# Stacked query and key rows: three stores in final order and one load of 96 rows, in place of one store and six loads of 16 rows

## The chip, the core and the metric

The kernel runs on one core of one Trainium2 chip. The metric is the device time of one execution in microseconds (us). Five engines work side by side, each with its own queue of instructions: TensorE (PE: matmuls; PEld: its weight loads), VectorE (DVE), ScalarE (ACT), GpSimd (POOL) and SyncE (SP). SP computes nothing here. It waits for semaphores and issues all transfers (DMAs), which sixteen DMA engines carry out. Engines and transfers wait for one another through semaphores only; a transfer adds 16 to its semaphore when it has landed.

## The reference, cut to what is computed

One Perceiver block over `x` [4, 256, 256] with a context [4, 4096, 256]. `ln` is a layer norm without weights.

```python
def reference(x, ctx, ...):
    x = x + xattn(ln(x), ctx)      # one head of width 256 over 4096 context tokens
    x = x + attn(ln(x))            # 16 heads of width 16, causal, three heads re-weighted by region
    x = x + soft_moe(ln(x))        # 64 experts with 32 slots each
    return x

# attn, per batch element and head h:
qkv = h @ c_attn_w + c_attn_b
scores = q @ k.T / sqrt(16)        # causal mask, softmax
attn = softmax(scores)             # heads 0 to 2: times 1.6 in one third of the tokens, normalised again
out = (attn @ v) @ c_proj_w + c_proj_b
```

The change lies in how `q` and `k` of the second step get from their projection to the score matmuls.

## The kernel before

Three blocks of code follow one another: `cross_attention`, `self_attention` and `soft_moe`. At the end of a block all five engines meet before any of them starts on the next one (line 202 is the head of the first).

**Why rows are stacked.** A projection value is split into three bf16 parts: high (ACT, `high_part`), middle (DVE forms the rest, ACT rounds it, `middle_part`) and low (POOL, L407 in cross-attention and L1073 in self-attention; semaphore `low_g`). The kernel sums six products of parts for a score. A head is only 16 wide, so it lays six rows of parts for each of the 16 dimensions on 96 partitions (`STACK` = 6, `ROWS` = 96), and one matmul over 96 partitions (L1163 and L1171, in `score`) sums all six products. `Q_STACK` and `K_STACK` name the part in each of the six places. Heads 0 to 2 have three more rows, which DVE fills.

**Eight stages.** `qk_stage(s)` gives for s = 0 to 7 a tile of 128 output columns (query tile 0, key tile 2, query tile 1, key tile 3) and a half of the tokens (s // 4: 512 tokens, two batch elements). The projection leaves the parts of one stage on 128 partitions, [128, 3, 512] bf16, with partition p = 8 i + h for dimension i and head h of the tile. The score matmuls want dimension i on the partition and head h along it. The parts go through DRAM for this:

- `store_parts(s)` waits for `low_g` of the stage and stores all three parts in one transfer of 384 KB (L119), in pieces of 1 KB.
- `stack_rows(s)` waits until that store has landed (`parts_out0` or `parts_out1`) and issues six loads (L128) of 16 partitions, 128 KB each. Each partition receives 8 KB, which lie together in DRAM. They add to `rows_in{s}`.

**The order on SP** is written out by hand. In `cross_attention` it is store 0, loads 0, store 1, loads 1, store 2, loads 2, store 3, and then the end of the block; no stage's instructions are put before those of the stage ahead. In `self_attention` SP issues loads 3, then store 4, loads 4, store 5, loads 5, store 6, loads 6, store 7, loads 7, and after these the load of `phi_w` (L1044, 2 MB) for the third step. Every transfer goes through SP's one queue.

**Who waits.** PE waits for `rows_in` 0 and 1 as it enters self-attention, and for 2 and 3 before `score(2, 0)`. The main loop of self-attention runs over i = 0 to 15 (four batch elements times four groups of four heads). Iteration i transposes the probabilities of group i, mixes group i - 1, and computes the first part of the scores of group i + 3. `rows_in` 4 and 5 are waited for at i = 5, 6 and 7 at i = 7, and the load of `phi_w` at i = 8, where `transpose_phi` (L1227) begins. The projections of stages 4 to 7 stand in the loop at i = 0 to 3, and their low parts in POOL's iterations 1 to 4. The buffers of parts are different ones for each stage, so no engine waits for a store to land except SP.

Of the kernel before, what the change touches and what calls it, by code (L numbers as in the profile page):

```python
# [9 lines left out]
P = 128  # L10
# [4 lines left out]
DH = D // P  # L15
# [8 lines left out]
BF16 = mybir.dt.bfloat16  # L24
# [3 lines left out]
NH, HD, GH = 16, 16, 4  # L28
# [1 line left out]
HPH = P // HD  # L30
CG = 2 * HD
NPART = 3
Q_STACK = (0, 0, 1, 0, 2, 1)
K_STACK = (0, 1, 0, 2, 0, 1)
STACK = len(Q_STACK)
ROWS = STACK * HD
FOCUSED = 3
LOG_FOCUS = math.log(1.6)
HALF = B * S // 2
# [61 lines left out]
def qk_stage(s):  # L101

    return QK_TILES[s % 4], slice(s // 4 * HALF, (s // 4 + 1) * HALF)


def heads_of(rows):
    return slice((rows % DH) * HPH, (rows % DH + 1) * HPH)
# [7 lines left out]
def store_parts(sp, kept, qk_dram, parts, s):  # L115

    rows, _ = qk_stage(s)
    sp.wait_ge(kept.sem["low_g"], s + 1)
    sp.dma_start(qk_dram[rows, s // 4].rearrange("c p t -> p c t"), parts).then_inc(kept.sem[f"parts_out{s % 2}"], 16)  # L119


def stack_rows(sp, kept, qk_dram, q_rows, k_rows, s):

    rows, _ = qk_stage(s)
    sp.wait_ge(kept.sem[f"parts_out{s % 2}"], 16 * (s // 2 + 1))
    for r in range(STACK):
        to, part = (q_rows, Q_STACK[r]) if rows < DH else (k_rows, K_STACK[r])
        sp.dma_start(to[r * HD:(r + 1) * HD, heads_of(rows), :],  # L128
                     qk_dram[rows, s // 4, part].rearrange("(i h) t -> i h t", i=HD)).then_inc(kept.sem[f"rows_in{s}"], 16)


def focus_factor(dve, nc, kept, ident):
# [833 lines left out]
def self_attention(nc, x_sb, x_stats, x_mv, x_ve, x_rstd, ident, kept, disp, ones, qk_dram, phi_w):  # L966
# [4 lines left out]
    with ExitStack() as st:  # L971
        def sb(name, shape, dt=F32):
            return st.enter_context(nc.sbuf_tensor(name, shape, dt))
# [8 lines left out]
        parts = sb("qk_parts", [P, AHEAD, NPART, HALF], BF16)  # L982
# [43 lines left out]
        rows_in = [kept.sem[f"rows_in{k}"] for k in range(8)]  # L1026
# [85 lines left out]
        def _(pe):  # L1112
# [64 lines left out]
            def transpose(G):  # L1177
                g = G % NG
                pe.wait_ge(norm_g, 2 * G + 2)
                at_least(pe, pT_a, G)  # L1180
                at_least(pe, pT_v, 2 * G)
                for h in range(GH):
                    to = psT[h // 2][:, (h % 2) * S:(h % 2 + 1) * S]
                    nc.tensor.transpose(to[:, 0:P], eA[:, g, h, :], ident[:])
                    last = nc.tensor.transpose(to[:, P:S], eB[:, g, h, 0:P], ident[:])
                    if h % 2:
                        last.then_inc(t_mm, 1)
                for h in range(GH):
                    last = nc.tensor.transpose(psT[2][:, h * P:(h + 1) * P], eB[:, g, h, P:S], ident[:])
                last.then_inc(t_mm, 1)  # L1190
# [34 lines left out]
            def transpose_phi(k):  # L1225
                for j in range(4):
                    last = nc.tensor.transpose(psX[:, j * P:(j + 1) * P],  # L1227
                                               phi_nat[:, k // 2 * 4 + j, k % 2 * P:(k % 2 + 1) * P], ident[:])
                last.then_inc(phi_mm, 1)

            for s in range(2):
                pe.wait_ge(rows_in[s], 16 * STACK)
            for part in range(3):
                score(0, part)
            transpose_attended()
# [4 lines left out]
            for part in range(3):  # L1240
                score(1, part)
            for s in (2, 3):
                pe.wait_ge(rows_in[s], 16 * STACK)
            score(2, 0)
            for i in range(GROUPS):
                if i + 2 < GROUPS:
                    score(i + 2, 1)
                    score(i + 2, 2)
                if i == 0:
                    pe.wait_ge(attT_a, B)  # L1250
                    pe.wait_ge(values_v, 2)
                    pe.wait_ge(xadd_v, QT * B)
                transpose(i)
                if i == 0:
                    transpose_second()
                if i == 8:
                    pe.wait_ge(phi_in, 16)
                    pe.wait_ge(out_v, 1)
                    transpose_phi(0)
                if i == 9:  # L1260
                    pe.wait_ge(phi_a, 1)
                    transpose_phi(2)
                if i in (11, 12):
                    pe.wait_ge(phi_a, i - 9)
                    transpose_phi(2 * i - 18)
                if i + 3 < GROUPS:
                    if i == 5:
                        for s in (4, 5):
                            pe.wait_ge(rows_in[s], 16 * STACK)
                        pe.wait_ge(frows_v, 10)  # L1270
                    if i == 7:
                        for s in (6, 7):
                            pe.wait_ge(rows_in[s], 16 * STACK)
                    score(i + 3, 0)
                if i == 1:
                    pe.wait_ge(values_v, 3)
                if i:
                    mix(i - 1)
                if i == 0:
                    pe.wait_ge(h2T_a, B)  # L1280
                    project_qk(4)
                if i in (1, 2, 3):
                    pe.wait_ge(rest_v, i + 4)
                    project_qk(i + 4)
                if i == 4:
                    pe.wait_ge(rest_v, 8)
                    project_v(3)
                if i == 5:
                    pe.wait_ge(values_v, 4)
                    project_out(0)  # L1290
                if i == 8:
                    pe.wait_ge(phi_v, 1)
                    transpose_phi(1)
                if i == 9:
                    pe.wait_ge(phi_v, 2)
                    project_out(1)
                if i == 10:
                    pe.wait_ge(out_v, 2)
                    transpose_phi(3)
                if i in (11, 12):  # L1300
                    pe.wait_ge(phi_v, i - 8)
                    transpose_phi(2 * i - 17)
                if i == 13:
                    pe.wait_ge(phi_a, 4)
                    project_out(2)
                if i >= GROUPS - 2:
                    pe.wait_ge(exp_a, 2 * GH * GROUPS)
                    transpose_normed(i - GROUPS + 2)
# [689 lines left out]
def perceiver_block(nc, x, ctx, Wq, bq, Wk, bk, Wv, bv, Wo, bo, c_attn_w, c_attn_b, c_proj_w, c_proj_b,  # L1998
                    phi_w, phi_b, expert_w, expert_b, out):
    SL = phi_w.shape[0]  # L2000
    with ExitStack() as st:
        x_sb = st.enter_context(nc.sbuf_tensor("x_sb", [P, TT, D], F32))
        x_stats = st.enter_context(nc.sbuf_tensor("x_stats", [P, TT, 6], F32))
        x_mv = st.enter_context(nc.sbuf_tensor("x_mv", [P, TT, 2], F32))
        x_ve = st.enter_context(nc.sbuf_tensor("x_ve", [P, TT], F32))
        x_rstd = st.enter_context(nc.sbuf_tensor("x_rstd", [P, TT], F32))
        ident = st.enter_context(nc.sbuf_tensor("ident", [P, P], F32))
        front = st.enter_context(nc.sbuf_tensor("front", [P, DH * SL], F32, side="right"))
        back = st.enter_context(nc.sbuf_tensor("back", [P, DH * SL], F32, side="right"))
        phib = st.enter_context(nc.sbuf_tensor("phib", [P, SL], BF16, side="right"))  # L2010
        wide = st.enter_context(nc.sbuf_tensor("wide", [P, TT * D], F32, side="right"))
        turned = st.enter_context(nc.sbuf_tensor("turned", [P, DH, B * S], F32, side="right"))
        bank = [st.enter_context(nc.psum_tensor(f"ps{i}", [P, 512], F32)) for i in range(8)]
        qk_dram = nc.dram_tensor("qk_parts_dram", (2 * DH, 2, NPART, P, HALF), BF16).ap()
        phi_dram = nc.dram_tensor("phi_parts_dram", (NPART, SL), BF16).ap()
        with ExitStack() as until_moe:
            kept = carried_tensors(nc, until_moe, bank, front, back, phib, wide, turned)
            cross_attention(nc, x_sb, x_stats, x_mv, ident, kept, x, ctx, Wq, bq, Wk, bk, Wv, bv, Wo, bo,
                            c_attn_w, c_attn_b, c_proj_w, c_proj_b, phi_b, qk_dram, phi_dram)
            disp = st.enter_context(nc.sbuf_tensor("disp", [P, TT, SL], F32))  # L2020
            ones = st.enter_context(nc.sbuf_tensor("ones", [P, P], BF16))
            self_attention(nc, x_sb, x_stats, x_mv, x_ve, x_rstd, ident, kept, disp, ones, qk_dram, phi_w)
        soft_moe(nc, x_sb, x_stats, x_mv, x_ve, x_rstd, ident, kept, disp, ones, expert_w, expert_b, out)
# [22 lines left out]
```

## Time and profile before

| | |
|---|---|
| time, median of 3 runs (all) | 675.2 us (675.18, 675.20, 678.64) |
| time of the profiled execution | 674.29 us |
| its span, from the first instruction to the last | 672.5 us |
| busy: PE, PEld, DVE, ACT, POOL | 608.6, 474.9, 397.4, 347.9, 249.5 us |
| mean granted TensorE clock | 0.962 of full |
| moved by DMA | 52.48 MB, 78 GB/s over the span |

The profiled execution lies 0.9 us below the median, and 1.8 us of it lie outside the span. Positions below are us from the start of the span. The shares of busy time are means over three blocks with different limits; the timelines and the stretches between 279 and 374 us are those in which this change's transfers run.

### The profile page before, as it was taken

The page shows a single profiled execution, that of the slowest core. Times are in us where ns is not written, and L with a number is a line of the kernel's source. Part 1 is how long each engine was busy: PE and PEld are TensorE (multiplying, and loading weights), DVE is VectorE, ACT ScalarE, POOL GpSimd, SP SyncE. Part 2 cuts the span into 40 slices and gives each one's busy share as a digit, 9 for nine tenths or more (in the row PEclk, how much of TensorE's full clock was granted, in tenths as well). Part 3 has the DMA queues.
Part 4 walks back from the last instruction along what each step waited for, and adds up shares of the span by engine and source line. Part 5 has one row for each costly group of instructions (what it writes and reads, how often), then busy time and mean ns, then how long its engine had stood idle before and what let it go on. Part 6 is the DMA issues. An engine that isn't in the chain of part 4 may idle for free. (4 is left out here: it accounts for less than half of the span.)

```text
span 672.5 us, 10468 instructions
## 1 busy us (share of the span) xinstructions
PE 608.6 (91%) x3740; PEld 474.9 (71%) x3740; DVE 397.4 (59%) x797; ACT 347.9 (52%) x1051; POOL 249.5 (37%) x206
## 2 busy tenths in 40 slices
PE   6998999999999998988985899899999876689998
PEld 5887999899989987866663674344448643358887
DVE  4756566666667664626774786968883578244000
ACT  2545444444444536633894783488885457741210
POOL 1442252232223243124586571333644159155000
PEclk9989999999999998998898999999999996789999
DMA  7223122112211210275188104000007048660000
GB/s 258 64 95 110 33 67 91 64 48 93 66 64 47 80 48 2 56 137 91 40 142 170 58 2 126 1 0 1 0 0 169 20 132 274 200 209 8 17 17 23
DMA packets 37000, 52.48 MB, mean 78 GB/s; under 512 B 4307, under 2 KB 31827, under 8 KB 36182
## 3 DMA queue, kind: packets, MB, share of 16 engines
q1 hardware_dynamic: 36950, 51.82, 28.2%
q8 instruction: 30, 0.49, 0.3%
q14 instruction: 20, 0.16, 0.1%
HBM read 47.60 MB, written 4.21 MB: 77 GB/s over the span
## 5 line engine op out<-in xcount | busy, mean ns | idle before, releaser
L379 POOL TENSOR_TENSOR ctx_lo<-front,ctx_hi 128x1024 fp32r<-128x1024 f32 x32 | 76.3, 2388 | 157.8 <-DVE ctx_hi L800 135.9
L485 PE MATMUL ps<-ctx_hi,pT_hi 128*128 128x256 f32 x256 | 75.5, 295 | 0.7 <-DVE pT_lo L815 0.7
L815 DVE TENSOR_TENSOR pT_lo<-ps,pT_hi 128x512 fp32r<-128x512 f32 x64 | 41.2, 686 | 56.1 <-ACT pT_hi L673 56.1
L487 PE MATMUL ps<-ctx_hi,pT_lo 128*128 128x256 f32 x256 | 72.6, 283 | 0.0
L486 PE MATMUL ps<-ctx_lo,pT_hi 128*128 128x256 f32 x256 | 72.5, 283 | 0.0
L650 ACT CAST ctxT_hi<-ps 128x512 fp32r<-128x512 f32 x64 | 34.5, 593 | 64.2 <-PE ps L442 64.2
L1711 PE MATMUL ps<-front,turned 128*128 128x512 f32 x128 | 63.5, 618 | 0.0
L1825 ACT ACTIVATE comb<-comb,cneg 128x64 f32<-128x64 f32 x160 | 62.8, 399 | 0.0
L1803 PE MATMUL ps<-front,comb 128*128 128x256 f32 x256 | 57.9, 387 | 0.0
L1658 POOL TENSOR_TENSOR disp<-disp,dinv 128x512 f32<-128x512 f32 x32 | 33.5, 1048 | 57.1 <-DVE dinv L1905 57.1
L1803 PEld LDWEIGHTS ps<-front,comb 128*128 128x128 f32 x256 | 49.5, 195 | 7.2 <-issue 0.4
L673 ACT CAST pT_hi<-ps 128x512 fp32r<-128x512 f32 x64 | 34.3, 588 | 36.0 <-PE ps L467 36.0
L485 PEld LDWEIGHTS ps<-ctx_hi,pT_hi 128*128 128x128 f32 x256 | 49.2, 192 | 1.4 <-DVE pT_lo L815 1.1
L486 PEld LDWEIGHTS ps<-ctx_lo,pT_hi 128*128 128x128 f32 x256 | 49.3, 193 | 0.1
L487 PEld LDWEIGHTS ps<-ctx_hi,pT_lo 128*128 128x128 f32 x256 | 49.1, 192 | 0.0
L792 DVE TENSOR_TENSOR ctxT_lo<-ps,ctxT_hi 128x512 fp32r<-128x512 f32 x64 | 41.2, 685 | 7.5 <-ACT ctxT_hi L650 7.1
L454 PE MATMUL ps<-ctxT_hi,qk_hi 128*128 128x512 f32 x128 | 43.0, 418 | 2.8 <-issue 2.0
L1669 POOL TENSOR_TENSOR comb<-comb,cinv 128x512 f32<-128x512 f32 x32 | 39.9, 1271 | 15.1 <-DVE cinv L1918 15.1
L1405 DVE TENSOR_REDUCE nmax<-ps 128x2 f32<-128x512 f32 (+1 forms) x48 | 31.9, 672 | 15.6 <-PE ps L1173 8.2
L454 PE MATMUL ps<-ctxT_lo,qk_hi 128*128 128x512 f32 x128 | 40.2, 396 | 0.0
L454 PE MATMUL ps<-ctxT_hi,qk_lo 128*128 128x512 f32 x128 | 40.2, 395 | 0.0
L467 PE MATMUL ps<-ident,wide 128*128 128x128 f32 x256 | 34.5, 278 | 3.7 <-ACT wide L664 3.5
(227 smaller groups left out, 1390.5 us busy)
## 6 DMA issues: line engine op xcount, KB each, us to landing
front<-in_ctx_dram SPq DMA_DIRECT2D x32, 512.0 KB, 3.3
back<-in_L_ffn_expert_w_dram SPq DMA_DIRECT2D x11, 1024.0 KB, 5.5
turned<-in_L_ffn_expert_w_dram SPq DMA_DIRECT2D x5, 1024.0 KB, 5.4
disp<-qk_parts_dram SPq DMA_DIRECT2D x24, 128.0 KB, 4.3
disp<-in_L_ffn_phi_w_dram SPq DMA_DIRECT2D x1, 2048.0 KB, 11.0
front<-in_L_ffn_expert_b_dram SPq DMA_DIRECT2D x4, 512.0 KB, 10.5
qk_parts_dram<-scores SPq DMA_DIRECT2D x4, 384.0 KB, 5.7
front<-qk_parts_dram SPq DMA_DIRECT2D x12, 128.0 KB, 4.4
```

Of the source, the lines that this page charges most:

```text
L379: nc.gpsimd.tensor_tensor(ctx_lo[:, cols], ctx_in_sb[:, c % SLOTS, :], ctx_hi[:, cols].bitcast(F32), ALU.subtract).then_inc(split_g, 1)
L454: last = nc.tensor.matmul(pS[q][:], a[:, dh, q * P:(q + 1) * P], k[:, c % 2, dh, :], start=step == 0, stop=step == 5)
L467: last = nc.tensor.transpose(to[q][:, j * P:(j + 1) * P], probs[:, c % 2, q, j * P:(j + 1) * P], ident[:])
L485: nc.tensor.matmul(pO[q][:, 0:D], pT_hi[:, c % 2, q, cols], hi, start=c == 0 and j == 0, stop=False)
L486: nc.tensor.matmul(pO[q][:, 0:D], pT_hi[:, c % 2, q, cols], lo, start=False, stop=False)
L487: last = nc.tensor.matmul(pO[q][:, 0:D], pT_lo[:, c % 2, q, cols], hi, start=False, stop=c == NCH - 1 and j == J - 1)
L792: nc.vector.tensor_tensor(ctxT_lo[:, c % 2, dh, :], ctx_banks(c, alone)[dh][:], ctxT_hi[:, c % 2, dh, :].bitcast(F32), ALU.subtract).then_ ...
L815: nc.vector.tensor_tensor(pT_lo[:, c % 2, q, :], probs_banks(c, alone)[q][:], pT_hi[:, c % 2, q, :].bitcast(F32), ALU.subtract).then_inc(p ...
L1669: nc.gpsimd.tensor_tensor(part, part, cinv[:, c, :].unsqueeze(1).broadcast_to([P, EB, NS]), ALU.mult).then_inc(cmul_g, 1)
L1711: last = nc.tensor.matmul(psL[u % 4][:], hT[:, c, t * P:(t + 1) * P], phiT[:, c, cols], start=False, stop=c == DH - 1)
L1803: last = nc.tensor.matmul(psY[t][:, 0:HID], comb[:, t, s * P:(s + 1) * P], mixed[:, s, :], start=s == 0, stop=s == ST - 1)
L1825: nc.scalar.activation(column, column, ACT.Exp, bias=cneg[:, c, p:p + 1], accum_out=csum[:, c, p:p + 1]).then_inc(cslot_a, 1)
```

## The change

The scratch tensor in DRAM has six slots per stage instead of three, in the order in which the rows are wanted. `store_parts` now issues three stores on the same queue. For a query tile they hold the high part three times, the middle part twice and the low part once (a source that repeats by a step of zero). For a key tile they hold parts 0 to 2, 0 to 1 and 0. The three stores hold 384, 256 and 128 KB, 768 KB in all, again in pieces of 1 KB. `stack_rows` waits for all three and issues one load of 96 partitions, 768 KB, in place of six. The order of the six places is a new one, but the six products are the same ones. PE's waits ask for 16 instead of 96. Nothing else is changed: the order of the stages on SP, the buffers and the work of the other engines are the same.

```diff
--- before.py
+++ after.py
@@ -30,9 +30,7 @@
 HPH = P // HD
 CG = 2 * HD
 NPART = 3
-Q_STACK = (0, 0, 1, 0, 2, 1)
-K_STACK = (0, 1, 0, 2, 0, 1)
-STACK = len(Q_STACK)
+STACK = NPART * (NPART + 1) // 2
 ROWS = STACK * HD
 FOCUSED = 3
 LOG_FOCUS = math.log(1.6)
@@ -116,17 +114,22 @@
 
     rows, _ = qk_stage(s)
     sp.wait_ge(kept.sem["low_g"], s + 1)
-    sp.dma_start(qk_dram[rows, s // 4].rearrange("c p t -> p c t"), parts).then_inc(kept.sem[f"parts_out{s % 2}"], 16)
+    first = 0
+    for r in range(NPART):
+        count = NPART - r
+        part = parts[:, r:r + 1, :].broadcast_to([P, count, HALF]) if rows < DH else parts[:, 0:count, :]
+        sp.dma_start(qk_dram[rows, s // 4, first:first + count].rearrange("r p t -> p r t"),
+                     part).then_inc(kept.sem[f"parts_out{s % 2}"], 16)
+        first += count
 
 
 def stack_rows(sp, kept, qk_dram, q_rows, k_rows, s):
 
     rows, _ = qk_stage(s)
-    sp.wait_ge(kept.sem[f"parts_out{s % 2}"], 16 * (s // 2 + 1))
-    for r in range(STACK):
-        to, part = (q_rows, Q_STACK[r]) if rows < DH else (k_rows, K_STACK[r])
-        sp.dma_start(to[r * HD:(r + 1) * HD, heads_of(rows), :],
-                     qk_dram[rows, s // 4, part].rearrange("(i h) t -> i h t", i=HD)).then_inc(kept.sem[f"rows_in{s}"], 16)
+    sp.wait_ge(kept.sem[f"parts_out{s % 2}"], 16 * NPART * (s // 2 + 1))
+    to = q_rows if rows < DH else k_rows
+    sp.dma_start(to[0:ROWS, heads_of(rows), :],
+                 qk_dram[rows, s // 4].rearrange("r (i h) t -> (r i) h t", i=HD)).then_inc(kept.sem[f"rows_in{s}"], 16)
 
 
 def focus_factor(dve, nc, kept, ident):
@@ -1229,7 +1232,7 @@
                 last.then_inc(phi_mm, 1)
 
             for s in range(2):
-                pe.wait_ge(rows_in[s], 16 * STACK)
+                pe.wait_ge(rows_in[s], 16)
             for part in range(3):
                 score(0, part)
             transpose_attended()
@@ -1240,7 +1243,7 @@
             for part in range(3):
                 score(1, part)
             for s in (2, 3):
-                pe.wait_ge(rows_in[s], 16 * STACK)
+                pe.wait_ge(rows_in[s], 16)
             score(2, 0)
             for i in range(GROUPS):
                 if i + 2 < GROUPS:
@@ -1266,11 +1269,11 @@
                 if i + 3 < GROUPS:
                     if i == 5:
                         for s in (4, 5):
-                            pe.wait_ge(rows_in[s], 16 * STACK)
+                            pe.wait_ge(rows_in[s], 16)
                         pe.wait_ge(frows_v, 10)
                     if i == 7:
                         for s in (6, 7):
-                            pe.wait_ge(rows_in[s], 16 * STACK)
+                            pe.wait_ge(rows_in[s], 16)
                     score(i + 3, 0)
                 if i == 1:
                     pe.wait_ge(values_v, 3)
@@ -2011,7 +2014,7 @@
         wide = st.enter_context(nc.sbuf_tensor("wide", [P, TT * D], F32, side="right"))
         turned = st.enter_context(nc.sbuf_tensor("turned", [P, DH, B * S], F32, side="right"))
         bank = [st.enter_context(nc.psum_tensor(f"ps{i}", [P, 512], F32)) for i in range(8)]
-        qk_dram = nc.dram_tensor("qk_parts_dram", (2 * DH, 2, NPART, P, HALF), BF16).ap()
+        qk_dram = nc.dram_tensor("qk_parts_dram", (2 * DH, 2, STACK, P, HALF), BF16).ap()
         phi_dram = nc.dram_tensor("phi_parts_dram", (NPART, SL), BF16).ap()
         with ExitStack() as until_moe:
             kept = carried_tensors(nc, until_moe, bank, front, back, phib, wide, turned)
```

## Rows read from the trace of the kernel before

**Rows 1.** The chain that ended last: first piece (start us, us, what).
```profile
410.82 0.37 PE ps L1709
```

**Rows 2.** SyncE timeline, end of cross-attention (start us, us, line, operation, count).
```profile
279.80 0.36 SPq L119 DMA_DIRECT2D qk_parts_dram<-scores  x1
...
285.25 0.38 SPq L119 DMA_DIRECT2D qk_parts_dram<-scores  x1
290.73 2.62 SPq L128 DMA_DIRECT2D back<-qk_parts_dram  x6
...
299.43 2.62 SPq L128 DMA_DIRECT2D front<-qk_parts_dram  x6
302.09 0.42 SPq L119 DMA_DIRECT2D qk_parts_dram<-scores  x1
```

**Rows 3.** PE timeline at the change of blocks; in brackets idle before, and releaser.
```profile
299.13 0.28 PE L487 MATMUL ps<-ctx_hi,pT_lo 128*128 128x256 f32 x1
303.16 0.58 PE L1163 MATMUL ps<-back,front 99*128 99x128 bf16 x4 [3.75 <-PEq L202]
```

**Rows 4.** SyncE timeline in self-attention.
```profile
331.70 0.38 SPq L119 DMA_DIRECT2D qk_parts_dram<-qk_parts  x1
334.19 2.86 SPq L128 DMA_DIRECT2D disp<-qk_parts_dram  x6
...
342.55 2.62 SPq L128 DMA_DIRECT2D disp<-qk_parts_dram  x6
...
351.03 3.89 SPq L128 DMA_DIRECT2D disp<-qk_parts_dram  x6
...
359.72 2.62 SPq L128 DMA_DIRECT2D disp<-qk_parts_dram  x6
362.38 0.42 SPq L1044 DMA_DIRECT2D disp<-in_L_ffn_phi_w_dram  x1
```

**Rows 5.** PE timeline in self-attention, around the waits for rows.
```profile
350.47 0.39 PE L1163 MATMUL ps<-disp 99*128 99x128 bf16 x4 [1.22 <-DMA disp<-qk_parts_dram]
...
359.26 0.60 PE L1189 MATMUL ps<-ident,eB 128*128 128x128 f32 x4
367.67 0.58 PE L1163 MATMUL ps<-disp 96*128 96x128 bf16 x4 [7.81 <-DMA disp<-qk_parts_dram]
...
373.44 0.66 PE L1227 MATMUL ps<-ident,disp 128*128 128x128 f32 x4 [0.62 <-DMA disp<-in_L_ffn_phi_w_dram]
```

**Rows 6.** VectorE timeline, first maximum after the long wait.
```profile
368.72 0.69 DVE L1405 TENSOR_REDUCE nmax<-ps 128x4 f32<-128x512 f32 x1 [5.76 <-PE ps L1167]
```

**Rows 7.** GpSimd timeline: operations that release stores.
```profile
289.51 1.17 POOL L407 TENSOR_TENSOR scores<-scores 128x512 bf16<-128x512 f32 x1 [4.29 <-ACT scores L692]
...
336.00 1.16 POOL L1073 TENSOR_TENSOR qk_parts<-qk_rest,qk_parts 128x512 bf16<-128x512 f32 x1 [1.47 <-ACT qk_parts L1322]
...
341.75 1.16 POOL L1073 TENSOR_TENSOR qk_parts<-qk_rest,qk_parts 128x512 bf16<-128x512 f32 x1 [1.75 <-ACT qk_parts L1322]
...
347.23 1.16 POOL L1073 TENSOR_TENSOR qk_parts<-qk_rest,qk_parts 128x512 bf16<-128x512 f32 x1 [0.77 <-ACT qk_parts L1322]
```

**Rows 8.** Stretches: busy us (and count) by engine, granted TensorE clock, DMA share, GB/s.
```profile
303.00:305.00 2.00, 1.84 (x10) 1.12 (x11) 1.52 (x4) 0.00 (x0) 1.55 (x4) 0.53 1.08 131
305.00:307.00 2.00, 2.00 (x10) 1.89 (x9) 1.33 (x3) 0.51 (x2) 0.00 (x0) 0.62 0.72 155
331.70:334.20 2.50, 2.50 (x27) 2.11 (x28) 1.95 (x4) 2.12 (x9) 2.50 (x2) 1.00 0.47 164
367.60:369.00 1.40, 1.33 (x9) 0.66 (x13) 0.28 (x1) 0.00 (x0) 0.00 (x0) 0.50 1.09 348
```

**Rows 9.** DMA issues: count, KB each, median us from issue to landing.
```profile
front<-in_ctx_dram SPq DMA_DIRECT2D x32, 512.0 KB, 3.3
back<-in_L_ffn_expert_w_dram SPq DMA_DIRECT2D x11, 1024.0 KB, 5.5
...
disp<-in_L_ffn_phi_w_dram SPq DMA_DIRECT2D x1, 2048.0 KB, 11.0
```

## Prediction

> **What bounds the kernel now.** I start with the chain that ended last. Its first piece lies at 410.82 us [rows 1], behind everything that the change touches. So the chain says nothing on this change, except that a gain or a loss before 410 us reaches the end only if all engines carry it to there. Next come the waits of TensorE, where three have to do with this traffic. The first is at the change of blocks: PE's last matmul of cross-attention ends at 299.41, its next starts at 303.16 after 3.75 us idle, released by the meeting of the engines [rows 3]. SyncE's timeline tells who came last: its loads of stage 2 begin at 299.43, and its store of stage 3 is issued until 302.51 [rows 2]. SyncE, not PE, ends that block, and 0.65 us later PE starts. The second and third are in self-attention: 1.22 us at 350.47 for the rows of stages 4 and 5, and 7.81 us at 367.67 for those of 6 and 7. Another 0.62 us at 373.44 is for the load of phi_w, which stands behind the rows in the same queue [rows 5].
>
> SyncE's timeline from 331.70 to 359.72 [rows 4] shows a closed ring: store, wait until landed, loads, next store. From one group of loads to the next it takes 8.36, 8.48 and 8.69 us, 8.5 in the mean. The low parts that release the stores are ready at 337.16, 342.91 and 348.39 [rows 7], so from the third store on it is not POOL that sets the pace. The reader is to see that SP's ring sets PE's arrival at 367.67.
>
> **What one turn of the ring consists of.** The store of stage 4 runs with nothing else in flight. From issue to the loads behind its landing it takes 2.5 us [rows 4], and its DMA share is 0.47 of 2.5 us [rows 8], so it occupies the DMA engines for 1.2 us and 1.3 us are fixed (some 0.5 before, 0.8 behind). A turn of 8.5 us is then 1.3 fixed, 1.2 store and the rest, 6.0 us, for the six loads ahead of it in the queue. That is 768 KB at only 130 GB/s.
>
> **The change, part by part.**
>
> *Stores.* Twice the bytes in the same pieces of 1 KB: 2.4 us of the DMA engines instead of 1.2, plus 1.2 per turn. A lone store lands after 3.7 us instead of 2.5. The three issues take 1.3 us of SP instead of 0.42; behind a load they hide under its transfer, at the end of the block they don't. For the repeating source and the second write stream no row exists. The lower bound is 0 more than by bytes; the upper one is three stores that don't overlap, 2.5 us each by the lone store, 5.0 us more than one instead of 1.2, so 3.8 beyond the bytes per turn. SP issues them without a wait between, and the phi_w load runs at 348 GB/s just behind other transfers [rows 8], so I take 0. At the upper bound a turn would be 2.5 us longer than now and the time beyond the slowest rival; I give that 1 in 30, inside its chance.
>
> *Load.* One issue of 0.42 us in place of six in 2.62 us. Its 768 KB cost between 3.15 us (1024 KB to 128 partitions land in 5.5 us [rows 9]; less 1.3 fixed leaves 4.2, times 0.75) and 6.0 us, if 96 partitions in one load drain no faster than six groups of 16. If the rate falls with the partitions, 96 for 128, it is 4.2. The 512 KB loads of the context give less still: 3.3 less 1.3, times 1.5, is 3.0. I take 3.5, near the large loads, because here too all DMA engines get several rows.
>
> The Trainium skill, "SBUF — State Buffer", section "Door 1: The DMA port swizzle", says that partitions 0 to 15 reach 4 of 16 ports and get some 109 GB/s; that would be 7.2 us for the six loads, where the trace gives 6.0, so it fits roughly. By its port table 64 of the 96 rows share 8 ports, which by its rate per port makes an estimate of 2.4 us for the new load, and of 664 us for the kernel.
>
> *A turn* then takes 1.3 + 3.5 + 2.4 = 7.2 us instead of 8.5. In general it changes by (load + store) - 7.2: the change pays only if the load falls by more than the 1.2 us that the stores gain.
>
> **First place, the change of blocks.** Store 0 is issued at 279.80 [rows 2] and lands at 283.5. Load 0 follows at once. Store 1 is issued at 285.25 as before, while load 0 still runs, so the turn holds: landed at 290.7 (before 290.73). The low part of stage 2 is ready at 290.68 [rows 7]. Store 2 lands at 297.9 (before 299.43). Load and three stores are issued until 299.7, where SP ended at 302.51. PE's own end is 299.41. Gain 2.8 us, at most 3.1, when PE ends the block. Next is PE at once: rows 0 and 1 have landed at 295.5, and rows 2 and 3 land at about 310, before PE asks (315.4). The long idle time was followed by a granted clock of 0.53 and 0.62 over 4 us of busy PE [rows 8], (0.47 + 0.38) x 2 = 1.7 us at full speed lost. A gap of 1.22 us was followed by a full-speed matmul, 0.39 us against 0.58 [rows 5], so the loss may vanish; but some engines still idle longer. I take half, 0.8, with 0 and 1.7 as bounds.
>
> **Second place, rows 6 and 7 and phi_w.** Counted in the old positions from 331.70: store 4 lands at 335.4 (before 334.19, the one place that loses). Store 5 is behind load 4 in any case; landed 342.6. Store 6 (low part 342.91) lands at 349.8, store 7 at 357.0, against 359.72. Load 7 lands 1.3 + 3.5 later, at 361.8; PE started on it at 367.67. Gain 5.8 us. The rows of stage 5 land at 347.4, before PE asks at 349.25, so the wait of 1.22 goes too, and is part of the 5.8: PE then waits 3.2 us from 358.6 instead of 7.81. What holds next is phi_w: issued at 357.5 instead of 362.38, its 2048 KB run at 348 GB/s, 6.0 us, from the end of load 7 at 361.0, and land at 367.9, against 373.44. That is the smaller gain, 5.5 us. The cover of the other engines: VectorE had worked off its queue at 362.96 and idled 5.76 us before 368.72 [rows 6]; 1.22 of shift on top, and its cap is 7.0. After 374 us no row of this traffic is left, and the engines move on together with PE to the end of the block.
>
> **Sum.** 2.8 + 5.5 + 0.8 = 9.1 us off the profiled execution's 674.29, 665.2. The median of the runs is 0.9 higher: 666 us.
>
> **The rivals.**
>
> *Less gain (about 672).* The load costs 4.2 to 4.9 us, or the engines behind PE give a part back. Each us of load costs 2 us in the first place (two turns) and 4 in the second (three turns and the last load). At 4.2 us the gains are 1.4 and 2.7, 671 us; at 4.9 both are nil.
>
> *No change (675).* Load and store together cost as much as before, 7.2 us in a turn. Stores that cost 3.7 instead of 2.4 do it as well with a load of 3.5. For it speaks that the bytes grow from 1.15 to 1.54 MB per stage while the DMA share was already 0.8 or more; against it, that the share is of engines that move only 130 GB/s.
>
> *Slower (681).* The load is bound by its target as the six were: if the DMA engines walk through the 96 partitions in step, sixteen neighbours at a time, nothing of the rate changes and it costs 6.0 us. Then SP ends the first block 2.2 us later, and phi_w lands 4.5 us later: 6.7 more, 681 us. It decides from 5.5 us of load on, where the loss passes 0.5%. For it speaks that no row shows a load of 96 partitions; against it, that the loads of 128 partitions reach 250 GB/s, and they too must be walked through somehow.
>
> **Chances.** Forecast (663.5 to 670.5) 0.60; less gain 0.14; no change 0.11; slower 0.15. Half a per cent, 3.4 us, is about what these measurements can tell from no change. Less gain is still faster for the most part: faster 0.73, same 0.13, slower 0.14. The low end takes a load of 3.0 us and the full clock, both places at their caps: 3.1 + 7.0 + 1.7 = 11.8, 663.4, and a little for a cheaper phi_w wait, 662.5. The high end reaches through no change to 677. The likeliest case's own range is 663.5 to 670.5.
>
> **What would show it.** The load of 96 rows should land 4.8 us after issue alone (4.4 to 5.5; near 7.3 is the slower case) and a lone group of stores 3.7 us after its first issue. Turns in self-attention should be 7.2 us. SyncE's last issue of cross-attention should come near 299.7, PE's idle before its first L1163 at about 1 us instead of 3.75, and the clock of the next 4 us above 0.6. The wait of 1.22 should be gone, that of 7.81 at about 3, and one for phi_w of about 1 us should follow. What would make it wrong: stores that cost more than their bytes, a load near 6 us, or a wait of VectorE or ScalarE in PE's chain after 360 us that eats the second gain.

## The result and the profile after

The changed kernel takes 672.97 us (median of 20 runs, 666.14 to 680.44) where the kernel before takes 676.02 (20 runs, 671.09 to 681.20). The ratio is 0.9949, with a 95% interval of 0.9928 to 0.9971: a gain of half a per cent, some 3.4 us. (Two of the changed kernel's twenty executions, the two with the lowest granted clock, count as slow and are left out of the ratio.) Forecast were 9.1 us, 666 from 675.2; 675.2 times 0.9949 is 671.8. The change does what it was forecast to do in direction, and little more than a third of it in size. The profiled execution took 672.64 us, its span is 670.9 us.

Single runs of one kernel spread over 10 to 14 us, so the share of each step is read from the profiles, as distances. The first store is issued at 280.65 in the profile after, 0.85 us later than before, although nothing ahead of it was changed. All sums below therefore start at that store.

The chain of the kernel after begins with the start of soft MoE, as before [rows 1]:

```profile
407.69 0.37 PE ps L1712
```

From the first store to this point it is 127.04 us; before it was 131.02. That is 4.0 us less, close to the 3.4 of the runs.

**First place.** SyncE's timeline at the end of cross-attention (start us, us, line, operation, count), against [rows 2]:

```profile
280.65 1.56 SPq L121 DMA_DIRECT2D qk_parts_dram<-scores  x3
284.39 0.33 SPq L131 DMA_DIRECT2D front<-qk_parts_dram  x1
286.10 1.62 SPq L121 DMA_DIRECT2D qk_parts_dram<-scores  x3
291.55 0.33 SPq L131 DMA_DIRECT2D back<-qk_parts_dram  x1
291.92 2.17 SPq L121 DMA_DIRECT2D qk_parts_dram<-scores  x3
299.39 0.33 SPq L131 DMA_DIRECT2D front<-qk_parts_dram  x1
299.76 2.10 SPq L121 DMA_DIRECT2D qk_parts_dram<-scores  x3
```

The reader is to see a lone group of stores that takes 3.74 us until the load (3.7 forecast), then turns of 7.16 and 7.84 us (7.2 forecast), and last that three issues take 2.10 us and not 1.3 when a load is in flight. From the first store to the end of SyncE's part it is 21.21 us instead of 22.71, a gain of 1.5. PE's timeline there, against [rows 3]:

```profile
299.98 0.28 PE L490 MATMUL ps<-ctx_hi,pT_lo 128*128 128x256 f32 x1
302.54 0.39 PE L1166 MATMUL ps<-back,front 99*128 99x128 bf16 x4 [2.28 <-PEq L205]
```

The idle time is 2.28 us instead of 3.75, and SyncE still ends the block. The stretches behind it (busy us and count by engine, granted clock, DMA share, GB/s) show what became of the clock [rows 8]:

```profile
303.00:305.00 2.00, 1.94 (x14) 1.70 (x15) 1.75 (x4) 0.41 (x1) 0.90 (x2) 1.00 0.92 271
305.00:307.00 2.00, 2.00 (x11) 1.74 (x11) 0.55 (x2) 2.00 (x12) 0.12 (x1) 1.00 0.67 233
```

It stays at full, 1.00, where it had been granted 0.53 and 0.62. At `score(2, 0)`, 316.20 instead of 318.20, the place has gained 2.85 us in all: 1.5 by SyncE and the rest, 1.4, which I put down to the clock, of whose 1.7 the forecast had taken half; store 4 is issued 3.2 us earlier (forecast 3.6).

**Second place.** SyncE's timeline in self-attention, against [rows 4]:

```profile
329.33 1.44 SPq L121 DMA_DIRECT2D qk_parts_dram<-qk_parts  x3
334.61 0.33 SPq L131 DMA_DIRECT2D disp<-qk_parts_dram  x1
...
342.63 0.33 SPq L131 DMA_DIRECT2D disp<-qk_parts_dram  x1
...
350.82 0.33 SPq L131 DMA_DIRECT2D disp<-qk_parts_dram  x1
...
358.29 0.33 SPq L131 DMA_DIRECT2D disp<-qk_parts_dram  x1
358.66 0.43 SPq L1047 DMA_DIRECT2D disp<-in_L_ffn_phi_w_dram  x1
```

and PE's [rows 5]:

```profile
348.86 0.39 PE L1166 MATMUL ps<-disp 99*128 99x128 bf16 x4 [1.98 <-ACT eB L1342]
...
364.01 0.59 PE L1166 MATMUL ps<-disp 96*128 96x128 bf16 x4 [4.79 <-DMA disp<-qk_parts_dram]
```

From store 4 to PE's start on rows 6 and 7 it is 34.68 us where it was 35.97: 1.3 us gained, 5.8 forecast. The parts are the lone stores, 5.28 us instead of 3.7; the turns, 8.02, 8.19 and 7.47 instead of three times 7.2; and the last load, 5.72 us instead of 4.8. These miss by 1.6, 2.1 and 0.9 us, 4.6 in all, which with the 1.3 gives the 5.8 but for rounding. The wait for the rows of stages 4 and 5 was to be gone, and it is not. The profile puts the 1.98 us at 348.86 down to ScalarE, but load 5 (issued at 342.63) landed 6.14 us later, at 348.77, within 0.02 us of ScalarE's end. PE starts 0.09 us after that landing, as it does at 364.01 after the one at 363.92. In four of the runs below the profile names the rows here (1.38 to 2.21 us).

### The profile page after: what moved, and what is told of

Its sections match the earlier page's. It is cut to its first block and busy times, and to the rows that moved or that the text cites. A ratio compares the mean times of both kernels' runs of the same rounds, so it can differ in the third digit from the quotient of the medians.

```text
span 670.9 us, 10444 instructions
## 1 busy us (share of the span) xinstructions
PE 610.1 (91%) x3740; PEld 475.4 (71%) x3740; DVE 397.3 (59%) x797; ACT 348.2 (52%) x1051; POOL 249.7 (37%) x206
## 5 line engine op out<-in xcount | busy, mean ns | idle before, releaser
L1714 PEld LDWEIGHTS ps<-front,turned 128*128 128x128 f32 x128 | 22.1, 193 | 23.3 <-issue 23.3
```

The source lines that it names most:

```text
L1714: last = nc.tensor.matmul(psL[u % 4][:], hT[:, c, t * P:(t + 1) * P], phiT[:, c, cols], start=False, stop=c == DH - 1)
```

## The experiments

Two theories stood at first. The load theory: the load of 96 rows costs 4.2 us of the DMA queue in a turn and not 3.5. The store theory: the second half of the stored bytes costs more than its bytes do. Rival to both: other engines absorb what the ring gains. In the table "lone store" is the time from the first issue of stage 0 and of stage 4 to the loads behind it, "turns" are those of self-attention, "idle" is PE's at the change of blocks, "rows 6, 7" its wait for them, and the last time is that from the first store to the start of soft MoE. All but the ratio come from the one profiled execution of each kernel.

| kernel | ratio to before (95%) | lone store 0 / 4 | turns | idle | rows 6, 7 | to MoE |
|---|---|---|---|---|---|---|
| before | 1 | 2.59 / 2.49 | 8.36, 8.48, 8.69 | 3.75 | 7.81 | 131.0 |
| changed | 0.9949 (0.9928 to 0.9971) | 3.74 / 5.28 | 8.02, 8.19, 7.47 | 2.28 | 4.79 | 127.0 |
| e1, three stores, six loads | 1.021 (1.0155 to 1.0264) | 3.73 / 5.29 | 9.50, 10.14, 9.44 | 9.33 | 8.76 | 144.4 |
| e2, one store, one load | 0.9805 (0.9756 to 0.9855) | 2.59 / 2.46 | 5.96, 6.25, 6.48 | 0.48 | 0 | 120.7 |
| e3, one store, three loads | 0.983 (0.977 to 0.989) | 2.59 / 2.49 | 7.15, 7.10, 8.39 | 0.48 | 2.58 | 122.5 |
| e4, no ring in self-attention | 0.9808 (0.976 to 0.9856) | 3.72 / none | none | 2.06 | 0 | 120.8 |
| e5, one store of 768 KB | 0.9858 (0.983 to 0.9885) | 3.74 / 3.54 | 7.11, 8.07, 7.41 | 0.48 | 2.08 | 122.2 |
| e6, load in two by heads | 0.9919 (0.9891 to 0.9946) | 3.74 / 5.29 | 7.73, 7.88, 8.17 | 1.50 | 4.68 | 125.7 |
| e7, stores 6, 7 ahead | 0.9863 (0.9841 to 0.9886) | 3.73 / 5.28 | 8.19, 8.23 | 1.66 | 1.60 | 122.8 |
| e8, e3 with stores 6, 7 ahead | 0.9837 (0.9814 to 0.986) | 2.59 / 2.49 | 7.25, 7.39 | 0.48 | 0 | 120.5 |
| e9, forty waits on SyncE | 0.9959 (0.9935 to 0.9984) | 3.72 / 5.23 | 8.04, 8.24, 7.48 | 1.95 | 5.75 | 128.0 |
| e10, e7 and store 3 ahead | 0.9828 (0.9797 to 0.986) | 3.72 / 5.30 | 8.02, 8.07 | 0.51 | 2.56 | 121.4 |

**Three stores, six loads.** The stores of the change alone.

```diff
-    sp.dma_start(to[0:ROWS, heads_of(rows), :],
-                 qk_dram[rows, s // 4].rearrange("r (i h) t -> (r i) h t", i=HD))...
+    for r in range(STACK):
+        sp.dma_start(to[r * HD:(r + 1) * HD, heads_of(rows), :],
+                     qk_dram[rows, s // 4, r].rearrange("(i h) t -> i h t", i=HD))...
```

> Three stores of the changed kernel (768 KB), six loads of 16 rows of the kernel before. If the load of 96 rows is the mis-sized term (it costs 4.2 us in a turn and not 3.5) and stores cost what their bytes do, a turn of SyncE's ring in self-attention is 1.3 + 2.4 + 6.0 = 9.7 us, SyncE ends cross-attention 2 us or more after that of the kernel before, and the time is 1 to 1.5% above it (682 to 685 us). If the stores are the mis-sized term (0.7 us more than their bytes in each turn), a turn is 10.4 us and the time 2% above. If neither matters because the gain is absorbed by other engines, the time is within 0.5% of the kernel before.

SyncE's timeline in self-attention:

```profile
339.17 1.46 SPq L121 DMA_DIRECT2D qk_parts_dram<-qk_parts  x3
344.46 2.64 SPq L132 DMA_DIRECT2D disp<-qk_parts_dram  x6
...
353.96 2.63 SPq L132 DMA_DIRECT2D disp<-qk_parts_dram  x6
...
364.10 3.23 SPq L132 DMA_DIRECT2D disp<-qk_parts_dram  x6
...
373.54 2.64 SPq L132 DMA_DIRECT2D disp<-qk_parts_dram  x6
```

The turns are 9.50, 10.14 and 9.44 us, 9.7 in the mean, and the kernel is 2.1% slower. The 9.7 is the sum 1.3 + 2.4 + 6.0, where the store theory asked for 10.4: in a turn behind six loads the stores cost what their bytes do, and the store theory falls. (Two instruction packets, code that is loaded by DMA, run in the turn of 10.14.) The one number that it could claim is the lone store of stage 4, 5.29 us, to which I come below. The slow rival of the forecast, a load at 6.0 us beside doubled stores, is this kernel: it was put at 1% slower and measures 2.1%. The 2% was also what the store theory asked for, so here turns and time point to different theories. What the time has beyond the turns lies ahead of them: SyncE ends cross-attention 28.27 us after the first store instead of 22.71, PE idles 9.33 us there and starts at half clock (its first matmul takes 0.58 us instead of 0.39).

**One store, one load.** The load of the change alone. Its rows overlap in the 384 KB that are stored, so the scores are made of wrong rows.

```diff
+    near = bass.AP(tensor=stage.tensor, offset=stage.offset, ap=[[2016, ROWS], [1, HPH * HALF]])
+    sp.dma_start(to[0:ROWS, heads_of(rows), :].rearrange("p h t -> p (h t)"), near)...
```

> The single store of 384 KB of the kernel before, and one load of 96 rows of 8 KB whose source rows overlap, so that 768 KB are read from the 384 KB that were stored; the scores are made of the wrong rows, everything else is as before. Load theory: a turn is 1.3 + 1.2 + 4.2 = 6.7 us. Store theory: 1.3 + 1.2 + 3.5 = 6.0 us. In both the wait of 7.8 us for rows 6 and 7 falls to 2 us or none and the time is 1 to 1.5% below the kernel before. If the gain is absorbed by other engines instead, the ring gets as much shorter, but the time stays within 0.5% of that of the changed kernel.

SyncE's timeline in self-attention:

```profile
326.73 0.36 SPq L119 DMA_DIRECT2D qk_parts_dram<-qk_parts  x1
329.19 0.32 SPq L129 DMA_DIRECT2D disp<-qk_parts_dram  x1
332.21 0.36 SPq L119 DMA_DIRECT2D qk_parts_dram<-qk_parts  x1
335.15 0.32 SPq L129 DMA_DIRECT2D disp<-qk_parts_dram  x1
337.97 0.36 SPq L119 DMA_DIRECT2D qk_parts_dram<-qk_parts  x1
341.40 0.32 SPq L129 DMA_DIRECT2D disp<-qk_parts_dram  x1
343.45 0.36 SPq L119 DMA_DIRECT2D qk_parts_dram<-qk_parts  x1
347.88 0.32 SPq L129 DMA_DIRECT2D disp<-qk_parts_dram  x1
```

The turns, 5.96, 6.25 and 6.48 us, are no sum of costs: each store is issued when its low part is ready, 3.0, 2.8 and 2.1 us after the load, and no longer by the ring. In the first turn the store lands 2.94 us after its own issue, against 2.46 alone: when it began to move, 0.9 us after its issue, load 4 was nearly out of its way. The wait for rows 6 and 7 is gone, and the time is 1.95% below that of the kernel before. The next lines are the GB/s of forty slices of the 5 us from the issue of a load on, with the packets begun in them; first the changed kernel, with three stores issued right behind load 5 (342.63):

```profile
GB/s 0 0 0 0 0 0 0 262 262 131 0 328 0 66 131 262 131 262 262 131 0 459 131 590 66 262 197 197 459 131 66 197 262 197 270 328 229 148 303 320
DMA packets 215, 0.88 MB, mean 176 GB/s; under 512 B 14, under 2 KB 121, under 8 KB 121
```

then this kernel, its store issued 2.8 us behind load 5 (335.15):

```profile
GB/s 0 0 0 0 0 0 0 262 328 262 0 131 197 131 524 393 262 459 328 197 262 328 131 524 131 328 131 328 197 197 188 98 156 270 344 336 352 369 352 303
DMA packets 421, 1.10 MB, mean 220 GB/s; under 512 B 19, under 2 KB 325, under 8 KB 325
```

Both start to move in the eighth slice, 0.9 us after issue. The GB/s hold the stores' bytes too, but the sizes tell them apart: the load moves in 96 packets of 8 KB, the stores in packets of 1 KB. Of the 96, 94 (215 less 121) have begun 5.0 us after issue in the first, and all of them (421 less 325) in the second. In the packet records of the changed kernel the last of the 96 begins 4.19 us after issue for load 3, which has the queue to itself, and 4.22 us for load 0, whose stores come 1.7 us later. For the five loads with stores right behind them it is 4.74 to 5.47 us, 5.1 in the mean. The landings follow: 5.5 and 5.3 us after issue for loads 3 and 0, 5.4 to 6.1 for the five. So the packets of a load in the clear run for some 3.7 us (0.95 to 4.65 after issue, with the last packet's own time), and some 4.5 with stores issued right behind it (to 5.05 to 5.77). The 3.5 of the forecast was not far from the price in the clear; what it lacked was that the load and the stores of the next stage are in the queue together.

**One store, three loads.** No bytes are added, and no store: the query tiles' parts lie in reverse order. (The last two lines add a wait for ScalarE: the place of the high part of stage 2 now lies over scores that its exponentials must have read first.)

```diff
+        slots = slice(r, NPART) if rows < DH else slice(0, count)
+        sp.dma_start(to[first * HD:(first + count) * HD, heads_of(rows), :],
+                     qk_dram[rows, s // 4, slots].rearrange("r (i h) t -> (r i) h t", i=HD))...
...
+                if s == 2:
+                    act.wait_ge(exp_a, QT * NCH * LAST + QT * 6 + 1)
```

> One store of 384 KB as before, but the three parts of a query tile lie in reverse order, so that three loads of 48, 32 and 16 rows give all six places (the same six products). No bytes are added. If what makes a load slow is how few partitions it covers, the three together cost between 4.2 and 6.0 us, say 4.8, and a turn is 7.3 us; time 0.6 to 1% below the kernel before. If it is the number of loads, 3 of 6 would halve the way from 6.0 to 4.2: 5.1 and 7.6 us. Under the store theory a turn is 6.7 us, as no store is added.

The turns are 7.15, 7.10 and 8.39 us, 7.5 in the mean, between the two expectations. Two instruction packets (0.5 and 1.3 us long) run among the transfers of the turn of 8.39; without it, and with the three turns of cross-attention (7.54, 7.23, 7.24), the mean is 7.25, nearer to the 7.3 of the partitions than to the 7.6 of the number of loads. That is a hint and no more. What the run does tell is that the six places can be filled at 0.983 of the kernel before, with the bytes of the kernel before. It beats both kernels.

**No ring in self-attention.**

> The changed kernel, but the rows of stages 4 to 7 are loaded from the stored parts of stages 0 to 3 at the start of self-attention; stores 4 to 7 are left out, and batch elements 2 and 3 get the scores of 0 and 1. No ring in self-attention is left. If the ring is what holds PE there, the waits for rows 6 and 7 (4.8 us in the changed kernel) are gone and phi_w is there early; soft MoE begins 4 to 6 us earlier than in the changed kernel and the time is 0.7% below it. If the other engines absorb the gain, soft MoE begins less than 2 us earlier.

Without stores 4 to 7 (batch elements 2 and 3 get the scores of 0 and 1) soft MoE starts 120.8 us after the first store, 6.3 us earlier than in the changed kernel, and the time is 0.9808. So what the ring gives up does reach the end, and the rival that other engines absorb it falls. It also bounds the second place: there are about 6 us beyond what the change took.

**One store of 768 KB.** 

```diff
+    same = parts[:, 0:1, :].broadcast_to([P, STACK, HALF])
+    sp.dma_start(qk_dram[rows, s // 4].rearrange("r p t -> p r t"), same)...
```

> The changed kernel with one store of 768 KB in place of the three (the high part six times; the middle and low parts are left out of the scores). Bytes and pieces are the same, two issues per stage are gone. If the load is slow in the changed kernel (some 3.9 us where it took 3.0 with one store released later) because three stores are issued on top of it, a turn in self-attention falls from 7.9 to about 7.2 us and the wait for rows 6 and 7 from 4.8 to about 2.5 us. If it is the bytes and pieces behind it, the turn stays at 7.9. The lone store of stage 4 took 5.3 us where that of stage 0 took 3.7: if that hangs on 768 KB in the queue when code is loaded, it stays at 5.3; if on the number of issues, it falls to 3.7.

The time is 0.9858, against 0.9949 with three stores of the same bytes in the same pieces. SyncE's timeline and PE's first matmul of self-attention show two of the three places where it comes from:

```profile
327.54 0.36 SPq L118 DMA_DIRECT2D qk_parts_dram<-qk_parts  x1
331.08 0.32 SPq L127 DMA_DIRECT2D disp<-qk_parts_dram  x1
```

```profile
300.57 0.39 PE L1162 MATMUL ps<-back,front 99*128 99x128 bf16 x4 [0.48 <-PEq L201]
```

The lone store of stage 4 takes 3.54 us instead of 5.28. PE's idle time at the change of blocks is 0.48 us, because SyncE's last issue takes 0.43 us and not 2.10. The turns are 7.11, 8.07 and 7.41, 7.5 in the mean. That is not the expected 7.2, and the turns sort themselves by another thing than the number of issues. With cross-attention's, the two turns of this kernel whose store waited 1.7 to 1.9 us for its low part are 7.01 and 7.11, and the four with the store right behind the load (issued 0.4 to 0.6 us after it) 7.41 to 8.07, 7.7 in the mean; in the changed kernel it is 7.16 against five of 7.47 to 8.19, 7.85 in the mean. So a turn costs some 0.6 to 0.7 us more when the store is right behind the load, whether in one issue or in three. Over all six kernels with one load of 96 rows and 768 KB of stores it holds without an exception: seven turns with a late store take 6.96 to 7.16 us, twenty with a close one 7.41 to 8.24 (turns with six stores left out). The turns were sorted afterwards, and no run delays a store and changes nothing else.

**The load in two, by heads.**

> The changed kernel with the load split into two of 96 rows by 4 KB (four heads each). If a load is slow because each partition gets 8 KB in one run, so that few partitions are written at a time, two passes change little: 3.9 us, turn 7.9. If the piece per row is what matters, the load falls to 3.2 us and the turn to 7.3. One more issue costs 0.4 us of SyncE at the end of cross-attention. Time within 0.5% of the changed kernel under the first, 0.5% below it under the second.

The turns are 7.73, 7.88 and 8.17, 7.9 as with one load; the time, 0.9919, lies between the two expectations and its interval overlaps that of the changed kernel. In cross-attention the turns were shorter than with one load (6.87, 7.36 and 7.19 against 7.16, 7.84 and 7.71). I take the load's piece per row to be of little weight; the run does not settle it.

**Forty waits on SyncE.** The lone stores of stage 4 take 5.2 to 5.3 us in every kernel that issues three, and all but twelve of their packets have begun by 332.8 in the changed kernel. GB/s and packets from there to the load (332.8 to 334.6):

```profile
GB/s 0 0 0 0 0 0 0 0 0 0 0 23 0 0 23 0 23 0 0 23 0 23 0 23 0 23 23 23 23 0 0 0 0 0 0 0 0 0 0 0
DMA packets 12, 0.01 MB, mean 6 GB/s; under 512 B 2, under 2 KB 12, under 8 KB 12
```

Twelve packets, ten of them of 1 KB, trickle in, one at a time, and the third store lands 0.5 us behind the last of them, 4.3 us after its issue (2.7 at stage 0).

```diff
+            for _ in range(40):
+                sp.wait_ge(kept.sem["low_g"], 4)
```

> The changed kernel with forty waits on SyncE that are met already, put behind load 3, where SyncE has nothing to do for some 20 us. They change only where the code of stage 4 lies in SyncE's program. The three stores of stage 4 alone took 5.28 us until load 4 was issued in three profiles, where those of stage 0 took 3.74 and one store of 768 KB took 3.54. If SyncE waits for its own code behind the store's packets there, 5.28 falls to about 3.7 here, or shows up at another stage. If it is the third issue itself, 5.28 stays. Time within 0.3% of the changed kernel either way.

5.23 us stay, with SyncE's code moved by forty instructions, and the time, 0.9959, is that of the changed kernel. So the place of SyncE's code is not it. The trace shows what the twelve packets came behind. The profile lists one packet of an instruction queue there, code of 16 KB:

```profile
q8 instruction: 1, 0.02, 1.1%
```

In the changed kernel it runs for 0.94 us, from 332.40 to 333.34, and the first of the twelve begins at 333.32. With six loads it ends at 343.26, and the first late packet begins at 343.25; with forty waits it is 332.13 and 332.12. At stage 0, where the stores take 3.74 us, no instruction packet runs. So the late packets begin when a load of code ends; that they wait for it, on the DMA engine that carries it, is the plain reading, but the records don't name the engine and no run takes the load of code away. The forty waits didn't: it is there 2.8 us after the first store, so it need not be SyncE's code. One store of 768 KB has the same packet 3.0 us after its issue, when almost all its own have begun, and loses nothing. Why three stores still have packets to send on that engine stays open.

**Stores ahead.** Only the order on SyncE is changed.

```diff
-            for s in range(4, 8):
+            for s in (4, 5):
                 store_parts(...)
                 stack_rows(...)
+            for s in (6, 7):
+                store_parts(...)
+            for s in (6, 7):
+                stack_rows(...)
```

> The changed kernel with the order of SyncE in self-attention changed: store 6 and store 7 are both issued before load 6 and load 7. Nothing else moves. If the fixed part of a turn (start and landing, about 1.8 us) is lost time of the DMA queue, the last load lands some 2 us earlier: wait for rows 6 and 7 falls from 4.8 to about 3 us, time 0.2 to 0.4% below the changed kernel. If the queue is never empty, no change.

SyncE's timeline, and the waits of PE behind it:

```profile
335.23 0.33 SPq L131 DMA_DIRECT2D disp<-qk_parts_dram  x1
335.60 1.92 SPq L121 DMA_DIRECT2D qk_parts_dram<-qk_parts  x3
343.42 0.33 SPq L131 DMA_DIRECT2D disp<-qk_parts_dram  x1
343.79 4.91 SPq L121 DMA_DIRECT2D qk_parts_dram<-qk_parts  x6
351.65 2.51 SPq L131 DMA_DIRECT2D disp<-qk_parts_dram  x2
354.20 0.43 SPq L1051 DMA_DIRECT2D disp<-in_L_ffn_phi_w_dram  x1
```

```profile
361.41 0.38 PE L1170 MATMUL ps<-disp 96*128 96x128 bf16 x4 [1.60 <-ACT eB L1346]
...
367.02 0.66 PE L1234 MATMUL ps<-ident,disp 128*128 128x128 f32 x4 [2.14 <-DMA disp<-in_L_ffn_phi_w_dram]
```

Store 7 no longer waits for store 6 to land. Load 6 goes at 351.65 and load 7 at 353.84, 2.2 us later, where a further turn of 7.5 us would have put it near 359. The wait for rows 6 and 7 falls from 4.79 to 1.60 us. The profile puts the 1.60 down to ScalarE, but load 7 landed at 361.32, 0.09 us before PE starts, and in the next run, with the same order, it names the rows (2.56 us). Then PE waits 2.14 us for phi_w. The gain is larger than expected, 0.9863 against 0.9949: some 5 of the 7.5 us of a turn are saved in the queue, not only its fixed part. The turn in which the second group of stores is issued is no longer than before (8.23 against 8.19).

**Stores ahead twice.**

> The changed kernel with stores 6 and 7 ahead of loads 6 and 7 (0.986 of the kernel before) and also store 3 ahead of load 2, which is now issued behind the change of blocks. If SyncE's last issues still hold the change of blocks (PE idle 1.7 to 2.3 us there, 0.5 where SyncE is early), the idle time falls to 0.5 us and the time by 0.2 to 0.3%, to 0.983 of the kernel before. If the loads behind the change of blocks are late, PE waits for rows 2 and 3 instead and nothing is gained.

With store 3 ahead of load 2 as well, PE's idle time at the change of blocks is 0.51 us as expected, and no wait for rows 2 and 3 appears. The ratio, 0.9828 (0.9797 to 0.986), is where it was expected, but its interval overlaps that of the kernel with one change of order.

**One store, three loads, stores ahead.**

> One store of 384 KB and three loads of 48, 32 and 16 rows (0.983 of the kernel before), with stores 6 and 7 both ahead of loads 6 and 7. There store 7 waited for SyncE and not for its low part, so it can go 1 us earlier and its transfer runs without a turn of its own: the wait of 2.6 us for rows 6 and 7 should fall to about 0 and soft MoE start 2.5 us earlier, 0.979 to 0.981 of the kernel before. If other engines absorb it, 0.983 stays.

The wait of 2.58 us is gone, and soft MoE starts 2.0 us earlier in the profile, but the ratio, 0.9837, is that of the kernel without the new order. The two orders of this layout can't be told apart by their times.

## Why the prediction was wrong

**What bounds the kernel: right.** SyncE's ring and its last issues ahead of the change of blocks hold PE. Without the ring soft MoE starts 6.3 us earlier.

**A lone group of stores, 3.7 us: right at stage 0 (3.74), wrong at stage 4 (5.28).** The step was "SP issues them without a wait between (...) so I take 0". Three issues in place of one cost three things that bytes don't show: 1.7 us until the last store of stage 4 has landed (5.28 against 3.54 with one issue, the load of code being there in both), 0.8 us more of SyncE at the end of the block (2.10 us instead of 1.3, with 0.43 for a single one), and 0.64 to 0.76 us per issue right behind a load where 0.43 was taken. The bytes were priced right: 9.7 us for a turn with six loads. Of the 1.3 us fixed, the forecast put 0.5 before and 0.8 behind the transfer; the trace of before has 0.9 and 0.45, which changes no sum of a lone store.

**The load, 3.5 us of the queue: nearly right in the clear, wrong in the turn.** That is the term that was mis-sized most. A turn was the sum of load and store as if one followed the other for nothing. With the store right behind it the turn is 7.4 to 8.2 us, in the mean 7.85 in the changed kernel; with the store 1.7 us or more later it is 7.0 to 7.2. The turn of 7.2 that was forecast exists only where the low part is late; in self-attention stores 5 to 7 are all ready ahead of the ring (store 5 by the delay of the lone store: its low part is ready at 334.79, and load 4 goes at 334.61; with one store of 768 KB it waits, and the first turn is 7.11). Three turns at 0.7 are the 2.1 us. The last load takes 5.72 us until PE starts, and not 4.8. Most of that is no matter of neighbours: it landed after 5.63 us, with phi_w right behind it, but load 3, which has the queue to itself, after 5.48 (5.1 to 5.5 in five kernels). The sum of 3.5 and the 1.3 us of a store was too low for a load alone: its packets run for 3.7 us after the 0.95 at the start, and it landed 0.5 to 0.8 us behind the last of them.

**The sum.** The result is near the forecast's own rival "less gain": it gave 671 us for a load of 4.2 us in a turn, and 671.8 came out, with turns of 7.85 us that leave 4.15 for the load. That the totals are so near is in part luck. The second place gained 1.3 us and not the rival's 2.7, and the clock, which its 671 leaves out, gave back 1.4. It had a chance of 0.14, too little, as the trace of before showed no single load with a big store right behind it. The rivals' totals also stand on two bases: 671 is taken from the median, 681 from the profiled execution. And the DMA share of a turn, "0.8 or more" in the rival "no change", reads 0.76, 0.82 and 0.66 in self-attention.

**The clock: better than forecast.** The idle time of 2.28 us was followed by full clock, as one of 1.22 had been, and 1.4 of the 1.7 us came back. But in the run with forty waits an idle time of 1.95 us was followed by a matmul of 0.58 us, half clock. So this credit is not safe, and the half of it was a fair price.

**Phi_w: no longer a bound of its own.** It was forecast to hold the second place at 5.5 us of gain; rows 6 and 7 did, as they came later than forecast. It shows where the rows come earlier: 0.85 us with one store of 768 KB, 2.14 with the stores ahead.

**The port map.** By the section of the Trainium skill named in the prediction ("SBUF — State Buffer", "Door 1: The DMA port swizzle") the estimate for the load was 2.4 us. In the clear its packets ran for 3.7, so the size of the estimate doesn't hold here. In kind it agrees: 96 rows in one load beat six groups of 16 (6.0). But the number of loads changed with it, and no run separates the two.

## What to carry to other kernels

A transfer has two prices, one alone and one with its neighbour in the queue; where a ring issues the next store right behind a load, the sum of both prices was too low here, by 0.7 us in 7.2. Splitting a transfer into several issues is not free even when SyncE seems to have time: three stores instead of one, at the same bytes, took back 6 of 9.6 us (0.9949 against 0.9858). And before bytes are added to save issues, look at the order: here the rows needed neither more bytes nor six loads once the parts of one side lay in reverse, and issuing two stores ahead of their loads, on top of the change, gave more than the whole change had (0.9863 after 0.9949). That order alone, on the kernel before, was not run. And where the profile names an engine for the end of a wait, look at the landings too: twice here a load landed 0.09 us before PE started.

## What was not expected of the hardware

SyncE's time per issue is not fixed: in the changed kernel three stores take 1.44 to 1.62 us with nothing in flight or 1.7 us behind a load, and 1.9 to 2.3 us right behind a load of 96 rows. A large load starts to move 0.9 us after its issue. And the last of three stores on one queue can land 1.6 us later than its bytes account for, repeatably at one stage (the group takes 5.23 to 5.30 us in six kernels) and never at another (3.72 to 3.74): its last packets move one at a time, and they begin when a load of 16 KB of code ends, which itself ran for 0.94 us.
